# A macaron block on one Trainium2 core: the slots of the scan's moved pairs, a group mark on GpSimd, and two moved pairs in the last row

## What is computed

```python
x = x + 0.5 * ffn(layernorm(x))      # first phase, f1
x = x + mamba(layernorm(x))          # middle phase
x = x + 0.5 * ffn(layernorm(x))      # second phase, f2, same weights
```

```python
scores = sigmoid(x @ router_w.T); s = scores + bias
group_score = sum of the top 2 of s in each group of 4
inside = the 2 groups with the best group_score
topk = top 4 of (s where inside, else -1); tw = 2.5 * scores[topk] / sum
routed = sum_e tw_e * (silu(x @ gate_e) * (x @ up_e)) @ down_e
```

```python
h = exp(delta * A) * h + (delta * u) * B     # for each of the 16 states
y = sum_n h_n * C_n + D * u                  # then [y, z] @ W_out
```

## Time and profile before

| | us |
|---|---|
| median of 3 runs (lowest, highest) | 872.44 (870.86, 872.67) |
| the profiled execution's own time | 870.91 |
| its span, first to last instruction | 869.2 |
| busy in the span: PE / PEld | 836.9 / 639.7 |
| busy in the span: DVE / ACT / POOL | 690.4 / 557.8 / 642.8 |
| mean granted clock of TensorE | 0.995 |
| first and last scan start | 335.3 / 553.5 |

### The profile page before, as it was taken

How to read it: one execution, slowest core, us unless ns; L and a number is a source line. 1 busy time by engine, 2 the same in 40 slices (tenths; PEclk the granted TensorE clock), 3 DMA queues, 4 the chain that set the end, 5 groups by cost and what they waited for, 6 DMA issues and landing times. The chain is left out here.

```text
span 869.2 us, 12767 instructions
## 1 busy us (share of the span) xinstructions
PE 836.9 (96%) x3899; PEld 639.7 (74%) x3899; DVE 690.4 (79%) x1271; ACT 557.8 (64%) x1049; POOL 642.8 (74%) x476
## 2 busy tenths in 40 slices
PE   8999999999999999889999997999999999999997
PEld 7678778887877786566566665687887887788885
DVE  6969778776976578999999999887876977776664
ACT  6565565565566658878889893466575556555553
POOL 6958675776675767799998997856767677676755
PEclk9999999999999999999999998999999999999999
DMA  8733474454434252565465553435366435536440
GB/s 215 217 127 110 146 194 117 133 128 140 123 112 134 84 143 95 189 200 184 156 203 192 171 176 140 150 97 170 97 189 185 122 124 155 154 100 190 135 122 25
DMA packets 126421, 126.88 MB, mean 146 GB/s; under 512 B 59400, under 2 KB 83088, under 8 KB 126352
## 3 DMA queue, kind: packets, MB, share of 16 engines
q1 hardware_dynamic: 103648, 120.81, 45.7%
q10 hardware_dynamic: 22704, 5.25, 2.8%
HBM read 116.59 MB, written 9.44 MB: 145 GB/s over the span
## 5 line engine op out<-in xcount | busy, mean ns | idle before, releaser
L810 POOL TENSOR_TENSOR act_lo<-act,act_hi 128x512 fp32r<-128x512 f32 x288 | 372.1, 1297 | 188.8 <-ACT act_hi L921 186.9
L914 ACT ACTIVATE bank<-bank 128x512 f32<-128x512 f32 x252 | 146.7, 582 | 234.9 <-PE bank L1249 226.7
L1145 DVE TENSOR_TENSOR sg<-bank,c_ring 128x512 f32<-128x512 f32 x252 | 172.5, 684 | 97.7 <-ACT bank L914 95.3
L1245 PE MATMUL bank<-x_parts,w_hi 128*128 128x512 f32 x572 | 231.7, 405 | 3.3 <-DVE sg L1145 2.1
L1123 DVE SCALAR_TENSOR_TENSOR act<-sg,bank 128x512 f32<-128x512 f32 x288 | 197.8, 687 | 41.7 <-PE bank L1249 20.7
L1249 PE MATMUL bank<-x_parts,w_hi 128*128 128x512 f32 x572 | 226.1, 395 | 0.0
L1246 PE MATMUL bank<-x_parts,w_lo 128*128 128x512 f32 x572 | 226.1, 395 | 0.0
L921 ACT ACTIVATE act_hi<-act 128x512 fp32r<-128x512 f32 x286 | 178.1, 623 | 0.4 <-PE bank L1221 0.4
L1245 PEld LDWEIGHTS bank<-x_parts,w_hi 128*128 128x128 f32 x572 | 107.4, 188 | 36.5 <-DVE sg L1145 4.7
L1249 PEld LDWEIGHTS bank<-x_parts,w_hi 128*128 128x128 f32 x572 | 107.5, 188 | 26.0
L1246 PEld LDWEIGHTS bank<-x_parts,w_lo 128*128 128x128 f32 x572 | 107.5, 188 | 25.6 <-issue 1.7
(11 more groups left out here) (186 smaller groups left out, 996.6 us busy)
## 6 DMA issues: line engine op xcount, KB each, us to landing
c_ring<-c_dram SPq DMA_DIRECT2D x252, 256.0 KB, 3.6
c_ring<-c_dram SPq DMA_DIRECT2D x64, 512.0 KB, 4.5
b_slots<-c_dram SPq DMA_DIRECT2D x8, 512.0 KB, 3.8
y_dram<-out_t SPq DMA_DIRECT2D x56, 64.0 KB, 2.8
y_tok<-y_dram SPq DMA_DIRECT2D x14, 256.0 KB, 3.7
xt_dram<-xn ACTq DMA_DIRECT2D x40, 64.0 KB, 3.5
xt<-xt_dram ACTq DMA_DIRECT2D x10, 256.0 KB, 2.8
out<-x_sb SPq DMA_DIRECT2D x7, 256.0 KB, 2.5
```

Source lines behind the costliest of these rows:

```text
L810: self.nc.gpsimd.tensor_tensor(m["act_lo"][:, g % LAG], m["act"][:, g % ACTS], m["act_hi"][:, g % LAG].bitcast(FP32), ALU.subtract).then_i ...
L914: nc.scalar.activation(self.h_bank[:, g % 2], self.h_bank[:, g % 2], ACT.Silu).then_inc(self.sg_ready, 1)
L1145: nc.vector.tensor_tensor(m["sg"][:, g % 2], silu, weight, ALU.mult).then_inc(self.w_done, 1)
L1245: nc.tensor.matmul(dst, m["w_hi"][:, k, n, :], x_hi, start=True, stop=False)
```

## The change

It has three parts. Row 0's moved pair (6) uses slot 1 in place of slot 0: `MOVED[0]` becomes `(None, 6)`, and the helpers learn to skip None. Slot 0 is then used for the first time by row 1. The comparison that makes `g_in` moves from VectorE's `dve_route` to the end of GpSimd's `pool_groups`, for f2's first row alone. Row 7 gets two moved pairs, 2 in slot 0 and 4 in slot 1; the input of the second is made by GpSimd at n = 1 of row 7.

```diff
-MOVED = ((6,),) + ((4,),) * 7
+MOVED = ((None, 6),) + ((4,),) * 5 + ((4,), (2, 4))
 SLOTS = 2
+MULT_STEP = 1
...
-    POOL_STEPS, MORE_STEPS = 5, 2
+    POOL_STEPS, MORE_STEPS = 6, 2
...
         s.do(nc.gpsimd.tensor_tensor(by_group(g_rank), halves[:, :, :, 0], halves[:, :, :, 1], ALU.add))
+        s.settle()
+        s.do(nc.gpsimd.tensor_scalar(m["g_in"][:, 0:TT * GROUPS], g_rank, float(TOP_GROUPS), None, ALU.is_lt))
...
             s.do(nc.vector.tensor_reduce(g_rank, g_ge, AX.X, ALU.add))
-        s.settle()
-        s.do(nc.vector.tensor_scalar(g_in.rearrange("p (t g) -> p t g", t=nt), g_rank, float(TOP_GROUPS), None, ALU.is_lt))
-        if not by_pool:
+            s.settle()
+            s.do(nc.vector.tensor_scalar(g_in.rearrange("p (t g) -> p t g", t=nt), g_rank, float(TOP_GROUPS), None, ALU.is_lt))
             yield
...
     def slot_uses(self, i, n):
-        return sum(len(pairs) > n for pairs in MOVED[:i])
+        return sum(self.uses_slot(j, n) for j in range(i))
+
+    def uses_slot(self, i, n):
+        return n < len(MOVED[i]) and MOVED[i][n] is not None
...
     def load_slot(self, sp, i, n):
-        if n >= len(MOVED[i]):
+        if not self.uses_slot(i, n):
             return
-        earlier = [j for j in range(i) if len(MOVED[j]) > n]
+        earlier = [j for j in range(i) if self.uses_slot(j, n)]
...
                         if i == 0:
-                            self.load_slot(sp, 0, 0)
+                            self.load_slot(sp, 0, 1)
...
     def pool_input(self, pool, i, n):
-        if n >= len(MOVED[i]):
+        if not self.uses_slot(i, n):
             return
...
                 if i == 0 and n == 4:
-                    self.pool_input(pool, 0, 0)
-                if n == 1:
+                    self.pool_input(pool, 0, 1)
+                if i and n == MULT_STEP:
                     self.pool_input(pool, i, 1)
```

## The result

The changed kernel takes 866.59 us (median of 5 runs, 865.78 to 867.22), beside 870.86 us for the kernel before (5 runs, 869.83 to 872.67). The ratio is 0.9947 with a 95% interval of 0.993 to 0.9963, that is 3.2 to 6.1 us: 0.53% faster, 4.3 us between the medians, where 4.5 were forecast. The forecast of 867.9 was set against the earlier median of 872.44, which lies at the upper end of the runs of before; the forecast gain off 870.86 would be 866.3.

What follows compares the result with a forecast made beforehand. VectorE was taken to bound the middle phase and TensorE f2, joined in row 7. Gains of 1.76 (row 1) and 2.75 us (row 7) made 4.5, so 867.9 us from the 872.44 median; range 866.4 to 870.3.

Steps and rivals of the forecast that it cites:

- the price of part 1, 1.76 us: Row 1, scans 11 to 13: time lost behind the queue's wait for scan 6, all expected back; bounds 0 and 1.76 us.
- The term of 0.39: Row 1, scan 12 to scan 13: 3.87 us against 3.48 behind scan 6, so 0.39 us counted as lost to the backlog.
- The term of 1.37: Row 1, scan 11 to scan 12: 3.57 us against 2.20 for a bare scan, so 1.37 us counted as lost.
- The base, 872.44 us: Earlier median of the kernel before, from which the gain was taken to give 867.9 us.
- VectorE bounds the middle phase, TensorE f2, and the handover in row 7 links them: VectorE executes 29.28 of 30 us in the middle phase; f2 slides with TensorE's entry in row 7; last scan 4.9 us earlier.
- Part 2, 2.02 us: Row 7: with g_in made on GpSimd, VectorE starts L1031 at 530.28 in place of 532.30 us, 2.02 us earlier.
- the lower bound: Row 7, g_in on GpSimd: gain 0 if L1031 is held in the same way as first reader of g_in.
- Part 3, 1.12 us on VectorE: Row 7: VectorE loses input 58, 1.20 us less 0.08 of overlap, 1.12 us.
- The chain on GpSimd: Row 7: product 56 ends at 532.6 us, added input 534.95, product 57 537.3, product 58 539.65, low part 540.9, product 59 543.25.
- The sum in row 7, 2.75 us: VectorE gains 3.14 us, but TensorE meets product 59 and goes on 2.7 to 2.8 us earlier; 2.75 taken, bounds 0 and 3.14.
- The total, 4.5 us: Whole kernel: 1.76 us from row 1 plus 2.75 us from row 7.
- The rival of the clock: Row 7: TensorE's low clock stays, row 7 gains 0 to 2.2 us, total about 2.8, time 869.6 us; chance 0.12.

Runs made afterwards that it cites:

- old_wait: Changed kernel with the old wait put back: row 1's slot 0 load waits for scan 6, though that scan reads slot 1; 867.96 us, ratio 0.9965.
- p2_mark: Kernel before with only the g_in comparison moved from VectorE to GpSimd; 868.18 us, ratio 0.9971.
- mark_psum: Kernel before with the g_in comparison left on VectorE but its result written to PSUM in f2's first row; 868.40 us, ratio 0.9973.
- psum13: Kernel before with the change's moved pairs in rows 0 and 7, and the g_in comparison on VectorE writing to PSUM; 866.75 us, ratio 0.9949.
- mult2: Changed kernel with row 7's second moved input made one pair later, after product 57; 867.39 us, ratio 0.9959; run again 867.46 us, 0.9956.
- p3_pair: Kernel before with only row 7's moved pairs changed to 2 in slot 0 and 4 in slot 1; 870.91 us, ratio 1.0.
- parts13: Changed kernel with the g_in comparison back on VectorE, moved pairs as in the change; 869.52 us, ratio 0.9981.

## Where the prediction was wrong, and where it was right

- *The step that failed: the price of part 1, 1.76 us.* The wait in the queue is the mechanism, and old_wait shows it; the size was off. The term of 0.39, "From scan 12 to scan 13", was wrong: I put an idle spell down to a backlog because it stood behind it. With the backlog gone scan 13 still comes 3.85 us behind scan 12 (3.87 before), so this term measured 0.02. The term of 1.37 came back as 1.37 in the profile, but it was the largest of five such losses; their mean is 1.1. Part 1 measured 1.39 us of handover and 1.2 us between the medians, where 1.76 was the forecast. It was the upper bound, and nothing in the argument for it told an idle spell of VectorE's own from a wait.
- *The base, 872.44 us.* The median of three runs stood 1.6 us above that of five, 870.86. The forecast time of 867.9 is 1.3 us above the measured 866.59 for this reason, and the measured time lies only 0.2 us above the lower end of the range.
- *VectorE bounds the middle phase, TensorE f2, and the handover in row 7 links them.* Right: the last scan moved by 4.49 us, where 4.9 were forecast, the handover by 4.14, and from the second mark to the end are 304.9 and 305.4 us.
- *Part 2, 2.02 us.* Right to the hundredth in the profile (4.03 to 2.01), and the choice against the lower bound is now backed by p2_mark and mark_psum. Its value in the times, 2.7 us, lies above 2.02, with an interval of 1.6 to 3.6 us.
- *Part 3, 1.12 us on VectorE.* Measured 1.14. The chain on GpSimd came out as worked out: counted from the start of L1031, product 57 was to end after 7.0 us and product 59 after 13.0; they ended after 6.95 (532.91 + 2.36 - 528.32) and 12.8. TensorE meets product 59 at the sum of pair 59, as forecast.
- *The sum in row 7, 2.75 us.* Measured 4.14 - 1.39 (part 1) = 2.75 us. The passing on in parts, 3.16 us on VectorE and 2.75 at the handover, was right because product 59 was followed and not VectorE alone.
- *The total, 4.5 us.* 4.14 from mark to mark; the missing 0.4 is the term of scan 13. That the medians fell by 4.3 and so came within 0.2 of the forecast is in part luck: their interval, 3.2 to 6.1 us, does not tell 4.1 from 4.5.
- *The rival of the clock.* Its price was too high. In psum13, which has parts 1 and 3 and the comparison out of the way, the clock is 0.50 and 0.69 in row 7 and the handover still 224.39. The low clock cost about 0.4 us there, by which TensorE's spread came late, 0.27 in old_wait, and nothing in mult2 (225.03 at 0.62, 225.02 at 1.00). And the reason given against it did not hold: 1 us of idle was expected before TensorE's step and 2.42 were measured, with the clock at full, while mult2 with 2.43 us of idle fell to 0.62. That the clock was full in the first profile of the whole change was luck, though it did not decide: with 0.68 in 528 to 532 us the handover was 224.43. The prediction said that the low clock "cost nothing" before. For the kernel before that is true by a margin of 0.16 us, and the traces of p3_pair and parts13 make this margin the likely reason why part 3 brings nothing without part 2. Taken one by one the parts give 1.2, 2.7 and 0 us between the medians, together 3.9, beside 4.3 for all three; the order in which one adds them up sets what part 3 seems to be worth.

## What to carry to other kernels

A wait in a DMA queue cost here what stood behind it in the queue, not what it guarded. Look for such a wait, and give the first user of a buffer another buffer; the loads behind it move up. A tiny instruction whose time is a multiple of its own elsewhere, and which ends together with one of another engine, is worth more than its size (2.31 us against 0.19 here); it could move to the other engine, and as well its result could move to PSUM. An idle spell behind a backlog need not belong to it: look whether what the instruction needs has moved too. After taking work from the bounding engine, follow the next engine's queue by hand to the point of handover; the saving is what arrives there.

## What the runs showed of the hardware

The granted clock of TensorE in a stretch behind an idle spell of 1.9 to 2.4 us is not a property of the program: the same kernel shows 1.00 or 0.68 in 528 to 532 us, and another 0.62 or 1.00 in 532 to 536 us, in two executions each. VectorE has idle spells of 0.44 to 0.46 us for which no wait was found; one moved from scan 13 to scan 10 when eight instructions were added some 200 us earlier (149 to 164 us, against 369). A VectorE comparison of 128x16 from SBUF to SBUF took 2.31 us beside a GpSimd product of 2.35 us, and 0.18 us with its result in PSUM. The wait in the SP queue holds scan 12 by 0.97 to 1.37 us (3.17 to 3.57 less 2.20) in the five kernels that have it, 3.8 us less than product 6 waits for its load.
